# The last seven of 39 expert tiles cut from 256 rows to 128, in a fused attention and mixture-of-experts kernel

## What is computed

```python
var = mean(x * x, -1);  xn = rms_w * (x * rsqrt(var + EPS))
gate = xn @ wg_W + wg_b + (genre_embed @ gg_W + gg_b)
gate_w = softmax(gate);  topk_w, topk_i = top_k(gate_w, 2)      # two of 8 experts for each row
cw = sum(one_hot(topk_i, 8) * topk_w[..., None], -2)
h1 = relu(einsum('bsh,ehm->bsem', x, W1) + b1)                  # 256 -> 512
h2 = relu(einsum('bsem,emn->bsen', h1, W2) + b2)                # 512 -> 512
out_e = einsum('bsen,enh->bseh', h2, W3) + b3                   # 512 -> 256
x + einsum('bseh,bse->bsh', out_e, cw)
```

## Time and profile before

| | |
|---|---|
| time, three launches | 984.64, 988.95, 991.41 us (median 988.95) |
| profiled execution, its own time | 985.31 us |
| its span, first to last instruction | 983.5 us |
| mean granted TensorE clock | 0.974 |
| busy of the span | PE 93%, DVE 76%, POOL 63%, PEld 56%, ACT 54% |

### The profile page before, as it was taken

One profiled execution on the slowest core, in us unless ns is written; L12 is line 12 of the kernel. 1 busy time (PEld: TensorE's weight loads), 2 busy tenths in 40 slices (PEclk: granted clock), 3 DMA queues, 4 the chain that ended last, 5 costly groups with the idle time before them and its releaser, 6 DMA issues. The chain is left out here.

```text
span 983.5 us, 24019 instructions
## 1 busy us (share of the span) xinstructions
PE 910.8 (93%) x6978; PEld 548.8 (56%) x6979; DVE 743.0 (76%) x1546; ACT 536.0 (54%) x1104; POOL 622.0 (63%) x761
## 2 busy tenths in 40 slices
PE   6799999999999999998878998989999999999993
PEld 3233333333333343332314777878888888888882
DVE  7688889898998999899886886685655665655652
ACT  3167787788778777875677653223233233233230
POOL 4314345546556555532445699889988878788785
PEclk9799999999999999998989999999999999999997
DMA  6553171714518162450365896834334334333332
GB/s 214 103 87 77 35 117 56 133 53 89 131 35 163 55 102 64 79 98 13 120 184 161 258 254 180 184 56 73 63 57 55 44 55 55 44 56 54 44 57 30
DMA packets 106768, 93.10 MB, mean 95 GB/s; under 512 B 60025, under 2 KB 99321, under 8 KB 104385
## 3 DMA queue, kind: packets, MB, share of 16 engines
q1 hardware_dynamic: 92000, 71.98, 31.9%
q0 software_dynamic: 14304, 19.15, 12.3%
q10 hardware_dynamic: 384, 0.97, 0.3%
HBM read 49.46 MB, written 38.68 MB: 90 GB/s over the span
## 5 line engine op out<-in xcount | busy, mean ns | idle before, releaser
L1232 DVE TENSOR_REDUCE mx<-bank 128x1 f32<-128x512 f32 x512 | 327.4, 682 | 45.2 <-PE bank L802 40.3
L1122 ACT ACTIVATE arena<-bank 128x512 f32<-128x512 f32 x512 | 277.7, 596 | 70.7 <-PE bank L813 67.0
L1155 ACT ACTIVATE hf<-bank,small 128x256 f32<-128x256 f32 x316 | 133.6, 471 | 262.5 <-PE bank L987 216.5
L677 POOL TENSOR_TENSOR hl<-hf,hh 128x256 f16<-128x256 f32 x316 | 236.5, 1114 | 56.2 <-DVE y_dest L1471 40.8
L1454 DVE CAST hh<-hf 128x256 f16<-128x256 f32 x316 | 178.7, 597 | 114.1 <-ACT hf L1155 108.0
L987 PE MATMUL bank<-hh,arena 128*128 128x256 f16 x1248 | 210.8, 275 | 9.2 <-POOL hl L677 8.2
L802 PE MATMUL bank<-arena 48*128 48x512 f16 x512 | 167.0, 393 | 13.9 <-DVE mx L1232 10.7
L987 PE MATMUL bank<-hl,arena 128*128 128x256 f16 x624 | 171.7, 275 | 0.0
L813 PE MATMUL bank<-arena 49*128 49x512 f16 x512 | 163.2, 388 | 8.5 <-ACT arena L1122 5.8
L685 POOL DMA_INDIRECT out<-y,y_dest x78 | 128.5, 1648 | 20.7 <-issue 17.6
L987 PEld LDWEIGHTS bank<-hh,arena 128*128 x1248 | 122.6, 98 | 32.6 <-issue 14.6
(11 more groups left out here) (215 smaller groups left out, 982.0 us busy)
## 6 DMA issues: line engine op xcount, KB each, us to landing
raw<-in_we SPq DMA_DIRECT2D x16, 1024.0 KB
arena<-parts_dram SPq DMA_DIRECT2D x84, 128.0 KB
parts_dram<-arena SPq DMA_DIRECT2D x64, 128.0 KB, 3.7
xs<-in_pads SPq DMA_DIRECT2D x8, 816.0 KB
arena<-in_xT SPq DMA_DIRECT2D x8, 512.0 KB, 4.6
arena<-in_x SPq DMA_DIRECT2D x8, 512.0 KB, 5.9
out<-rows SPq DMA_DIRECT2D x8, 512.0 KB, 5.0
arena<-parts_dram SPq DMA_DIRECT2D x24, 64.0 KB, 3.0
```

What stands on the lines that cost most here:

```text
L677: nc.gpsimd.tensor_tensor(hl[which][:, par, m, :], hf[which][:, m, :], hh[which][:, par, m, :], ALU.subtract).then_inc(lo[which], 1)
L1122: nc.scalar.activation(pr[:, s % TT, n, :], b_bank[no % B_RING][:, :], ACT.Exp, scale=SCALE).then_inc(b_read, 1)
L1155: nc.scalar.activation(hf[which][:, m, :], layer[which][m // 2][:, m % 2 * TS:(m % 2 + 1) * TS], ACT.Relu, bias=bias[which][:, bass.ds(e, ...
L1232: V.tensor_reduce(mx[:, g % 2, s % TT, c:c + 1], a_bank[no % A_RING][:, :], X, ALU.max).then_inc(a_read, 1)
```

## The change

The last seven tiles (32 to 38) have 128 rows. Rows are shared out in units of 128: the expert's full early tiles (two units each), then its further pairs of units, then a single unit where one is left. 32 large tiles and 7 small ones hold 71 units, the worst case of 8192/128 + 8 − 1. The table has 24 entries (`ENTRIES`, three classes of 8 experts) for 39 tiles in place of 16 entries for 41 tiles; a sixth step of it comes in turn 11. Tile 39's layer 1, its loads and those of tile 40 are dropped. The loop has 8 passes (turns 15 to 30), and turns 31 to 38 are laid out one after the other. `load_tile` and `load_tag` still fetch 256 rows.

```diff
+LARGE = 2 * T // TS
+TILES_MAX = LARGE + NX - 1
+LOOPED = LARGE - 1
+ENTRIES = 3 * NX
+def rows_of(i):
+    return P if isinstance(i, int) and i >= LARGE else TS
+def results_of(tiles):
+    if not isinstance(tiles, int):
+        return tiles * 16 * SUB
+    return 16 * (SUB * min(tiles, LARGE // 2) + max(tiles - LARGE // 2, 0))
...
     def turns(engine, body):
         for i in range(UNROLLED):
             body(i, i % 2, i // 2 + 1)
         engine.wait_ge(late_set, 1)
-        with engine.Fori(0, (TILES_MAX - UNROLLED) // 2) as pair:
+        with engine.Fori(0, (LOOPED - UNROLLED) // 2) as pair:
             body(2 * pair + UNROLLED, 1, pair + UNROLLED // 2 + 1)
             body(2 * pair + UNROLLED + 1, 0, pair + UNROLLED // 2 + 2)
+        for i in range(LOOPED, TILES_MAX):
+            body(i, i % 2, i // 2 + 1)
...
         def take_hidden(which, i, par, nth=None):
+            n = rows_of(i)
             for m in range(MT):
                 pool.wait_ge(hi[which], i * MT + m + 1)
-                nc.gpsimd.tensor_tensor(hl[which][:, par, m, :], hf[which][:, m, :], hh[which][:, par, m, :],
+                nc.gpsimd.tensor_tensor(hl[which][:, par, m, 0:n], hf[which][:, m, 0:n], hh[which][:, par, m, 0:n],
...
-        def scatter_result(par):
-            for s in range(SUB):
+        def scatter_result(i, par):
+            for s in range(rows_of(i) // P):
...
-                xh, xl = (x_parts[1 - par][:, c, :, :] for c in range(2))
+                xh, xl = (x_parts[1 - par][:, c, :, rows_] for c in range(2))
...
         def final(i, par, e):
             after(pe, y_made, i)
-            for s in range(SUB):
+            for s in range(rows_of(i) // P):
...
         def body(i, par, nth):
             now = i if isinstance(i, int) else None
-            next_rank = rank_of(i + 1)
-            hidden(0, i + 1, 1 - par, next_rank, nth + par)
+            if now != TILES_MAX - 1:
+                hidden(0, i + 1, 1 - par, rank_of(i + 1), nth + par)
...
         def late_table(step):
...
+                chain(V.tensor_scalar(icount[:, :], icount[:, :], 1, None, ALU.arith_shift_right))
+                chain(V.tensor_copy(halves[:, :], icount[:, :]))
             elif step == 1:
...
+                for c, here in enumerate((first_, second_, third_)):
+                    running(ends[:, here], units[:, here])
...
             elif step == 2:
...
+                chain(V.tensor_scalar(limit[:, :], ends[:, 2 * NX - 1:2 * NX], 1.0 / SUB, float(LARGE), ALU.mult, ALU.min))
+                chain(V.scalar_tensor_tensor(unit[:, :], w["count"][:, 0:n], limit[:, 0:1], w["count"][:, 0:n], ALU.min, ALU.add))
             elif step == 3:
+                owner(unit, n, ENTRIES)
+            elif step == 4:
+                look_up(wide[:, :], rank, n, ENTRIES)
...
+            elif step == 5:
+                look_up(number[:, :], moved, n, ENTRIES)
```

More of the change, by code:

```diff
@@ L537, in body @@
             now, r = i if isinstance(i, int) else None, split_rank(i)
-            sp.wait_ge(tile_read, i + 2)
-            load_tile(i + 2, par)
+            if now is None or now + 2 < TILES_MAX:
+                sp.wait_ge(tile_read, i + 2)
+                load_tile(i + 2, par)
             if now != 0:
@@ L979, in hidden @@
                     pe.wait_ge(full_set[which], (i - 1) * MT + m + 2)
-                out = layer[which][m // 2][:, m % 2 * TS:(m % 2 + 1) * TS]
+                out = layer[which][m // 2][:, m % 2 * TS:m % 2 * TS + rows_of(i)]
                 c = slice(m * P, (m + 1) * P)
@@ L984, in hidden @@
                         pe.wait_ge(lo[0], i * MT + k + 1)
-                    ah, al = (xh[:, k, :], xl[:, k, :]) if which == 0 else (hh[0][:, par, k, :], hl[0][:, par, k, :])
+                    ah, al = (xh[:, k, :], xl[:, k, :]) if which == 0 else (hh[0][:, par, k, rows_], hl[0][:, par, k, rows_])
                     for n, (a, part) in enumerate(((ah, 0), (ah, 1), (al, 0))):
@@ L1154, in take_hidden @@
                     act.wait_ge(lo[which], (i - 1) * MT + m + 1)
-                nc.scalar.activation(hf[which][:, m, :], layer[which][m // 2][:, m % 2 * TS:(m % 2 + 1) * TS],
+                nc.scalar.activation(hf[which][:, m, 0:n], layer[which][m // 2][:, m % 2 * TS:m % 2 * TS + n],
                                      ACT.Relu, bias=bias[which][:, bass.ds(e, 1), m], scale=1.0 / WSCALE)\
@@ L1201, in body @@
             r, now = split_rank(i), i if isinstance(i, int) else None
-            take_hidden(0, i + 1, 1 - par, r)
+            if now != TILES_MAX - 1:
+                take_hidden(0, i + 1, 1 - par, r)
             if now == 2:
@@ L1392, in early_table @@
                 chain(V.tensor_tensor(rank[:, 0:NX], steps[:, :], upon[:, :], ALU.add))
-                chain(V.tensor_copy(rank[:, NX:2 * NX], rank[:, 0:NX]))
+                for c in range(1, 3):
+                    chain(V.tensor_copy(rank[:, c * NX:(c + 1) * NX], rank[:, 0:NX]))
             elif step == 4:
@@ L1400, in early_table @@
             elif step == 5:
-                owner(n, NX)
+                owner(w["count"], n, NX)
                 chain(V.tensor_copy(tables[0]["expert"][:, :], number[:, 0:n]))
@@ L1453, in take_hidden @@
                     dve.wait_ge(made[which + 1], (i - 1) * (MT if which == 0 else 1))
[L1454 removed]
+                nc.vector.tensor_copy(hh[which][:, par, m, 0:n], hf[which][:, m, 0:n]).then_inc(hi[which], 1)
                 if splits is not None and m % 2 == 1:
@@ L1460, in take_final @@
             dve.wait_ge(made[2], i + 1)
-            after(dve, y_out[par], (nth - 1) * 16 * SUB)
-            for s in range(SUB):
+            after(dve, y_out[par], results_of(nth - 1))
+            subs = rows_of(i) // P
+            for s in range(subs):
                 last = nc.vector.scalar_tensor_tensor(y[:, par, s, :], y_bank[:, s * E:(s + 1) * E], 1.0 / WSCALE,
@@ L1564, in body @@
                 late_table(4)
+            elif now == 11:
+                late_table(5)
             take_hidden(1, i, par, r)
```

67 lines of the change are left out of this document (37 added, 30 removed).

## The result

The changed kernel takes 975.13 us (median of 4 runs, 974.06 to 976.99) beside 988.31 for the kernel before in the same session (4 runs, 984.64 to 991.41): a ratio of 0.9882, interval 0.985 to 0.9915. It is faster, by 13.2 us where 16.25 were forecast. The profiled execution took 975.91 us, with a span of 974.1.

What follows compares the result with a forecast made beforehand. TensorE's matmuls bound turns 15 to 38 at 10.48 us, its sequencer nearly a second bound at 9.5. Savings of 11.9 + 4.65 − 0.3 = 16.25 us gave 969.1 profiled, 972.6 by the runs' median; range 967 to 978.

Steps and rivals of the forecast that it cites:

- The bound: Small turns on TensorE: set by its sequencer's register instructions and loads at 9.5 us, not by columns at 5.2 us.
- The turns: Turns 31 to 38 on TensorE: savings of 1.2 + 2.2 + 4.9 + 3.6 = 11.9 us.
- 3 x 0.75 + 2.1 + 4.1 + 1.05: Sequencer's own time of a turn: three loads of the expert's place, then register instructions of layers 1, 2, 3; 9.5 us.
- the lead put down to the sequencer: Sequencer enters turn 31 some 0.7 us ahead, then is 1.2 ahead again, shortening turn 32 to 8.3 us.
- The end: After the last matmul of layer 3 of tile 37: 4.65 us less of 19.8, with one sub-tile and two DMAs less.
- The late table: VectorE's table work grows by some 6 us, mostly hidden around turns 8 to 14: cost 0.3 us, bounds 0.2 and 6.
- A: Small turns: register instructions run closer together, GpSimd is next at about 6.9 us a turn; 16 us less, 957; 6%.
- the page's rule: Trainium skill's sustained 81 ns per weight load and matmul at 128 columns: small turn about 7.1 us, 14 us more gain.
- B: TensorE's granted clock falls in small turns, which take 10.4 us in place of 9.5: 5 us, 977.6; 12%.
- C: The late table's cover is thin: its 6 us come on the path in turns 8 to 11, 978.5; 8%.
- D: Code fetch stalls laid-out turns 31 to 38 by f each, costing 8f; 1001 at 3.5 us; 5% small f, 3% slower.
- E: Compiler keeps full width or engines wait for each other in turns 31 to 38: within 1% of before; 4%.

Runs made afterwards that it cites:

- Fixed weights: Changed kernel with the expert's place a constant 0 in the small tiles, no loads or register instructions for weights, output wrong there: 951.22 us, 0.9613.
- kept places: Changed kernel with the place of each tile's expert loaded once and kept in a register from turn 31 on: 967.66 us, 0.9794.

## Why the prediction was right, and where it was not

**The bound, right.** The step that decided, that narrow matmuls would run at the sequencer's pace, held: a turn of 9.7 us for 9.5, register instructions at 0.13, weights never the limit. Fixed weights and kept places moved the turn by what the count of its sequencer instructions says.

**The turns, 11.9 forecast, 10.3 measured.** The mechanism was right, the size of the turn a little off. The starts of layer 1 in the changed kernel, turn by turn, with layer 2 for turn 38 and the end of layer 3 of tile 37:

```
turn    31     32     33     34     35     36     37     38     end
us   885.51 895.40 905.00 913.91 923.60 933.32 943.06 952.71 959.29
```

Turns 34 to 37 take 38.8 us for 41.9: 3.1 saved, 3.9 forecast. In "3 x 0.75 + 2.1 + 4.1 + 1.05" each term held: the sequencer's rows of a small turn give 2.29 + 2.11 + 4.19 + 1.16 = 9.75 us. (The chain cuts the same turn elsewhere, at the ends of matmuls: gaps of 1.69 and stretches of 8.02.) Turns 31 to 33 give 3.1 (9.89, 9.60 and 8.91 us for 10.48), 4.4 forecast: the lead put down to the sequencer was too large, as layer 1 of tile 32 took 1.97 us with its gap and not 1.4, and turn 32 still has a large layer 3. Turn 38 gives 4.1 for 3.6.

**The end, 4.65 forecast, 5.0 measured.** Two DMAs less, one eviction, one product, a narrower subtraction (0.43 us, foreseen between 0.33 and 0.67).

**GpSimd, right in that it stays hidden.** Groups by line and shape, changed kernel, window 914 to 953, against the earlier trace rows:

```profile
L698 POOL TENSOR_TENSOR hl<-hf,hh 128x128 f16<-128x128 f32 x32 | 15.5, 623 | 17.4 <-DVE hh L1497 9.9 <-DVE y_dest L1515 7.5
```

The small subtraction was taken at 0.6 us, from half of "today's mean of 1.24". Both means misread the rows: the subtractions overlap in the profile, so the busy time counts, 145.1/196 = 0.74 us each before and 15.5/32 = 0.48 in small tiles. With the DMA GpSimd is busy 4.9 us of a small turn, where 6.4 were forecast. Neither binds at 9.7.

**The late table, 0.3 forecast, 2.2 measured: the term that was off.** "Step 5 falls before the casts, and GpSimd begins only later" counted VectorE's time and asked whether its casts come late, and it looked at GpSimd's work of the same turn, while the step runs beside GpSimd's turn before. What it left out is that a two-operand instruction of VectorE also holds up GpSimd, which bounds those turns: some 1.2 us beside step 3 and 0.9 beside step 5. The bound given (up to 6) held it.

**The balance.** 10.3 + 5.0 − 2.2 = 13.1 us, beside 13.2 and 13.6 in the two comparisons. The forecast of 972.6 is 2.5 under the measured 975.13.

**The rivals.** A (columns count) and the page's rule fell: the turn was 9.7, not 7. B fell: granted clock 1.00 in all small turns. C named the right place, with another mechanism (VectorE's time in place of GpSimd held up) and too large a size, 6 us for 2.2. D fell: 51 reads of code for 44, and no gap beyond the three loads'. E fell: widths are 128 in the trace.

A correction to the record: the rows named "turn 11" in the earlier trace rows belong to turn 12, as layer 1 of tile 13 starts at 678.19. Nothing hangs on it, as the pace is the same in both.

## What to carry to other kernels

Before tiles are made smaller, add up what the engine's sequencer does for one tile, register instructions and loads of values: it doesn't shrink with the tile, and here it ate 4.4 of the 5.2 us that a turn could have lost. Once it is the bound, an instruction that was free (the same table entry read three times) is worth removing; ask for it in the same change. Where VectorE works beside a GpSimd that is the bound, count the two-operand instructions by themselves, against its DMA issues too.

## What the runs showed of the hardware

A GpSimd subtraction of 128x256, 0.66 to 0.71 us alone, took 1.55 to 1.62 when a VectorE product of two f32 operands of 128x936 ran beside it, and an indirect DMA of GpSimd 2.52 in place of 1.62; that product, 1.12 alone, took up to 1.59. A VectorE sum over one operand of the same size (1.13 us) left the subtraction at 0.73 or less and the indirect DMA at 1.63. The Trainium skill (SBUF — State Buffer, Who interferes with whom) has this rule: a VectorE instruction with two inputs in SBUF contends with a GpSimd instruction that reads SBUF, while a reduction never does. The traces agree, with the numbers just given.

Kernels whose work up to the experts is the same came to them between 518.9 and 530.0 us. That spread of 11 us is five times the cost of the table; what sets it was not tried.
